# x loaded by pairs, a reordered beginning, and unread TensorE products, in an adaLN block on one core

## The chip, the cores and the metric

The kernel runs on one NeuronCore of one Trainium2 chip. The metric is the device time of one execution, in microseconds (us). Time before: 280.03 us, the median of 3 runs (278.7 to 280.95).

## The reference, cut to what matters

x has 16 batches ("blocks" below) of 256 tokens with 128 features. A condition vector gives each block a shift, a scale and a gate for attention and for the linear layer.

```python
mod = (_silu(c) @ wmod).reshape(16, 6, 1, -1)        # sa, ca, ga, sb, cb, gb
h = _layernorm(x) * (1 + ca) + sa
qkv = h @ W_qkv + b_qkv                              # 16 heads of 8 features
attn = softmax(einsum('bqhe,bkhe->bqhk', q, k)) / sqrt(128)
x = x + ga * (einsum('bihv,bvhd->bihd', attn, v) @ W_out + b_out)
h = _layernorm(x) * (1 + cb) + sb
x = x + gb * (quantised(h) @ quantised(w).T + bias)  # fp6 grid, blocks of 32
```

ga and gb are first pushed away from zero to at least 0.25 in magnitude.

## The kernel before, in words

All 16 blocks go through one software pipeline of `STEPS` (b = -2 to 18), each of 16 steps s. In step (b, s) TensorE computes the *second* scores of block b, head s (`scores2`, L1014, k as rows, into `ps_p2`), for which ScalarE takes the exponential (`exponentials`, L645), and the *first* scores of the head that lies LEAD = 20 steps ahead (`scores1`, L999, into the three banks of `ps_p1`), of which VectorE only takes each row's maximum (`maxima`, L822). The negated maxima are split by GpSimd (`split_max`), transposed by TensorE (L1058), copied to `maxT` by ScalarE (L637) and placed by two DMAs into two spare rows of `q_rows` (`place_max`, L409), so that the second scores come out with the maximum subtracted. Block 0's first scores thus begin at b = -2, s = 12; from there to b = 0 only first scores run (the lead phase).

For block c = b + 3, iteration b also prepares x: `transpose_x` (L1038), ScalarE's modulation into hT (`save_hT`, L615), q and k products (`project_qk`, L1051), ScalarE's copy (L626), GpSimd's split in a high and a low part (L515, L517). SyncE stores these parts to DRAM (`store_part`, L363) and loads them back in the layout that the scores want (`lay_out`: q_rows L375, k_rows L380; k_rows takes two DMAs, u = 0 and 1, for each half r). Blocks 0 and 1 are prepared ahead of the loop with `first_qk` (ScalarE, L620) and `first_low_part` (VectorE, L755). The LayerNorm statistics of x come from VectorE (`stats1`, L743, and `aggregate1`, L749 with L737 and L738), for block b + 5 in steps 6 and 7 of iteration b; those of blocks 3 and 4 in iterations -2 (s = 13, 14) and -1. Values (L1029), the output projection (L1082), LayerNorm 2 and the quantised linear layer (`transpose_hd` L1090, `linear` L1096) of a block follow in the next two iterations. The last block has a chain of its own (`..._last`; its last transposes L1120 and products L1124).

Each engine carries out its own list in order. SyncE's list is written by hand (L386 to L469): loads, the first stores and layouts, and then per iteration b: modb of block b + 1 (`load_modb`, L416), `place_max(b + 1, 0)`, the output of block b - 3 (L421), the two stores and the two layouts of block b + 3, `place_max(b + 1, 1)`. x is loaded in five transfers: blocks 0 and 1 by ScalarE, 2 and 3 early (L403), 4 and 5 behind the stores of block 1 (L435), and blocks 6 to 15 in one of 1280 KB ahead of the loop (L451). TensorE's list, ahead of its loop: the transpose of c, the modulation products, block 0's transpose and projections, block 1's transpose and projections, then the product of the 16 x 512 modulation rows (L1135), and `wf_d` and bias products (L1138, L1139), and block 2's transpose. ScalarE copies the modulation rows behind `first_qk` of block 1. VectorE carries out the weight's quantisation, the statistics of block 2, `first_low_part` of block 1, the operations on the modulation rows (L804 to L810), and the attention bias (L814).

Of the kernel before, what the change touches and what calls it, by code (L numbers as in the profile page):

```python
# [63 lines left out]
def adaln_block(nc, x, w_qkv, b_qkv, w_out, b_out, w_ffn, b_ffn, cond, w_mod, out):  # L64
# [4 lines left out]
    with ExitStack() as ctx:  # L69
# [147 lines left out]
        x_in = [sem("x0_in"), sem("x1_in"), sem("x2_x3_in"), sem("x4_x5_in"), sem("x_rest_in")]  # L217
# [99 lines left out]
        def x_ready(c):  # L317
            return (x_in[c if c < 2 else c // 2 + 1 if c < 6 else 4], 16)
# [47 lines left out]
        def lay_out(eng, c, kind, halves=range(2)):  # L366
# [4 lines left out]
            for r in halves:  # L371
# [5 lines left out]
                else:  # L377
                    for u in range(2):
# [8 lines left out]
        def _(sp):  # L387
# [15 lines left out]
            sp.dma_start(x_all[:, 2:4, :, :], x_tok[:, 2:4]).then_inc(x_in[2], 16)  # L403
# [24 lines left out]
            for r in range(2):  # L428
                lay_out(sp, 0, 0, (r,))
                lay_out(sp, 0, 1, (r,))  # L430
# [4 lines left out]
            sp.dma_start(x_all[:, 4:6, :, :], x_tok[:, 4:6]).then_inc(x_in[3], 16)  # L435
            sp.wait_ge(rows_ready, 1)
            sp.dma_start(mod_rows_dram, mod_rows[:, :, :].rearrange("b a n -> b (a n)")).then_inc(rows_stored, 16)
            for r in range(2):
                lay_out(sp, 1, 0, (r,))
                lay_out(sp, 1, 1, (r,))  # L440
            place_max(0, 0)
# [9 lines left out]
            sp.dma_start(x_all[:, 6:NB, :, :], x_tok[:, 6:NB]).then_inc(x_in[4], 16)  # L451
            for b in range(NB + 3):
# [14 lines left out]
                if has(b + 1):  # L467
                    place_max(b + 1, 1)
            sp.wait_ge(out_stored, 16 * NB)  # L469
# [125 lines left out]
        def _(act):  # L595
# [68 lines left out]
            first_qk(1, 0, q_full)  # L664
            first_qk(1, 1, k_full)
            act.wait_ge(rows_full, 1)
            act.activation(mod_rows[:, 1, :], rows_psum[:, 1, :], ACT.Copy)
            act.activation(mod_rows[:, 2, :], rows_psum[:, 2, :], ACT.Copy, bias=1.0).then_inc(rows_copied, 1)
            act.wait_ge(const_full, 1)
# [50 lines left out]
        def _(dve):  # L720
# [63 lines left out]

            dve.wait_ge(weights_loaded, 16 * 4)
# [12 lines left out]
            stats1(FIRST)  # L798
            aggregate1(FIRST)
            first_low_part(1, 0)  # L800
            first_low_part(1, 1)

# [10 lines left out]
            dve.wait_ge(wfT_copied, 1)  # L813
            dve.tensor_tensor(attn_bias[:, :], ps_post[:, E:2 * E], bout_bc[:, :], ALU.add).then_inc(const_ready, 1)  # L814
# [124 lines left out]

            for b in STEPS:  # L940
                for s in range(16):
# [20 lines left out]
                    if s == (13 if b == -2 else 6) and in_steps(b + 5):  # L962
                        stats1(b + 5)
                    if s == (14 if b == -2 else 7) and in_steps(b + 5):
# [15 lines left out]
        def _(pe):  # L980
# [260 lines left out]
```

## Time and profile before

| what | value |
|---|---|
| median of 3 runs | 280.03 us (278.7 to 280.95) |
| the profiled execution, own time | 277.82 us |
| its span in the profile | 275.8 us |
| TensorE busy | 256.1 us, 93% |
| VectorE busy | 232.6 us, 84% |
| ScalarE busy | 207.0 us, 75% |
| GpSimd busy | 185.8 us, 67% |
| moved by DMA | 35.45 MB, mean 129 GB/s |
| granted TensorE clock, mean | 0.945 |

The profile is of one execution; its times count from the start of the span. PE is TensorE (PEld its weight loads, which overlap it), DVE VectorE, ACT ScalarE, POOL GpSimd, SP SyncE; a q behind a name (SPq) is the engine's issuing of DMAs. "out<-in" names the tiles by the program's names without numbers, so `ps_p` stands for ps_p1, ps_p2 and ps_post or ps_pre where a line says so. The granted clock is a share of 2.4 GHz: 1.00, or 0.50 for 1.2 GHz. The recorded clock begins with its first event at 16.6 us, and a share of 1.00 before that is no reading.

### The profile page before, as it was taken

Reading aid. Unit: us, or ns where it says so; the run is one execution under the profiler, and the core shown is the slowest. Engines: PE = TensorE matmul, PEld = TensorE weight load, DVE = VectorE, ACT = ScalarE, POOL = GpSimd, SP = SyncE. Lnnn points to the kernel's source line nnn. Section 1 sums busy time; section 2 is a strip of 40 time slices with the busy share of each in tenths; the row PEclk is TensorE's granted clock in tenths of the full one; section 3 lists DMA queues with packets and bytes.
Section 4 is the critical chain, followed back from the end, with each engine's and each line's share of the span. In section 5 each row is a group of like instructions: output and inputs, shape, how many; then the busy total and the mean of one; then the engine's idle time right before and its main releaser. Section 6 shows DMA issues by size and latency. Waiting matters only on the chain.

```text
span 275.8 us, 7500 instructions
## 1 busy us (share of the span) xinstructions
PE 256.1 (93%) x2538; PEld 167.5 (61%) x2538; DVE 232.6 (84%) x597; ACT 207.0 (75%) x414; POOL 185.8 (67%) x384
## 2 busy tenths in 40 slices
PE   2789999999999999999999999999999989899952
PEld 2447656566666667666666666666767656565631
DVE  6679868889999999999999999999998978953264
ACT  5436867869797979888888889797979767878620
POOL 5724071558788878788887979797978653728450
PEclk9995559999999999999999999999999979999995
DMA  5476477555263536364626263726273440100001
GB/s 140 138 224 195 127 211 252 157 154 155 68 186 107 186 104 187 94 174 110 192 86 190 92 198 92 179 104 194 89 187 106 140 152 24 40 24 25 0 22 37
DMA packets 21205, 35.45 MB, mean 129 GB/s; under 512 B 3344, under 2 KB 16928, under 8 KB 19120
## 3 DMA queue, kind: packets, MB, share of 16 engines
q1 hardware_dynamic: 20592, 34.46, 42.5%
q10 hardware_dynamic: 576, 0.52, 0.6%
q8 instruction: 20, 0.33, 0.5%
q14 instruction: 17, 0.14, 0.2%
HBM read 23.93 MB, written 10.52 MB: 125 GB/s over the span
## 4 chain that ended last, share of the span: by engine, by line
PE 80%; DVE 6%; DMA 5%; SPq 3%; issue 3%; POOL 1%; ACT 1%; POOLq 0%; ACTq 0%; DVEq 0%
PE ps_p L999 29%; PE ps_o L1029 21%; PE ps_pre L1051 6%; PE ps_p L1014 4%; PE ps_post L1082 4%; PE ps_pre L1045 3%; PE ps_o L1068 3%; PE ps_post L1096 3%; PE ps_pre L1058 3%; DVE neg_max L822 2%; PE ps_pre L1038 2%; PE ps_post L1090 2%; DMA q_dram<-qk_parts 2%; PE ps_post L1076 1%; SPq L380 1%
## 5 line engine op out<-in xcount | busy, mean ns | idle before, releaser
L822 DVE TENSOR_REDUCE neg_max<-ps_p 128x2 f32<-128x512 f32 x256 | 164.2, 680 | 15.4 <-PE ps_p L999 14.0
L645 ACT ACTIVATE probs<-ps_p 128x512 f32<-128x512 f32 x256 | 139.2, 596 | 21.1 <-PE ps_p L1014 16.6
L999 PE MATMUL ps_p<-k_rows,q_rows 62*128 62x256 f32 x512 | 103.1, 324 | 2.8 <-DVE neg_max L822 1.6
L1014 PE MATMUL ps_p<-q_rows,k_rows 64*128 64x256 f32 x512 | 100.4, 315 | 1.5 <-DMA q_rows<-maxT 1.1
L999 PEld LDWEIGHTS ps_p<-k_rows,q_rows 62*128 62x128 f32 x512 | 74.2, 198 | 32.0 <-DVE neg_max L822 12.9
L1014 PEld LDWEIGHTS ps_p<-q_rows,k_rows 64*128 64x128 f32 x512 | 71.7, 190 | 5.2 <-ACT probs L645 2.8
L1029 PE MATMUL ps_o<-probs,v_aug 128*32 128x256 f32 x1024 | 70.0, 392 | 0.3 <-ACT probs L645 0.3
L1029 PEld LDWEIGHTS ps_o<-probs,v_aug 128*32 128x32 f32 x1024 | 27.1, 110 | 20.7 <-issue 1.6
L495 POOL CAST max_parts<-neg_max 128x16 fp32r<-128x16 f32 x32 | 6.4, 199 | 45.3 <-DVE neg_max L822 45.3
L517 POOL TENSOR_TENSOR qk_parts<-qk_full_sb,qk_parts 128x256 fp32r<-128x256 f32 x28 | 20.5, 731 | 2.3
L1051 PE MATMUL ps_pre<-hT,wqk_sb 128*128 128x256 f32 x56 | 19.2, 426 | 0.0
L637 ACT ACTIVATE maxT<-ps_pre 16x256 fp32r<-16x256 f32 x32 | 11.7, 365 | 6.6 <-PE ps_pre L1058 6.6
L626 ACT ACTIVATE qk_full_sb<-ps_pre,bqkv_col 128x256 f32<-128x256 f32 x28 | 13.2, 473 | 3.9 <-PE ps_pre L1051 3.8
L346 POOL TENSOR_TENSOR hq<-h,rs 128x256 fp8e4<-128x256 f32 x15 | 9.3, 617 | 8.7 <-DVE rs L868 8.7
L522 POOL TENSOR_TENSOR rstd<-ve,minus_half 128x2 f32<-128x2 f32 x16 | 11.2, 702 | 5.4 <-DVE ve L738 5.4
L515 POOL CAST qk_parts<-qk_full_sb 128x256 fp32r<-128x256 f32 x28 | 11.3, 403 | 5.3 <-ACT qk_full_sb L626 5.3
L329 POOL TENSOR_SCALAR xh<-x,nm,rstd 128x128 f32<-128x128 f32 x30 | 13.2, 452 | 1.6
L502 POOL TENSOR_TENSOR rstd<-ve,minus_half 128x2 f32<-128x2 f32 x16 | 11.2, 700 | 4.0 <-DVE ve L738 4.0
L354 POOL TENSOR_SCALAR xhat<-x_all,nm,rstd 128x128 f32<-128x128 f32 x28 | 12.3, 452 | 1.5
L550 POOL TENSOR_TENSOR x_res<-x_all,bias_b 128x256 f32<-128x256 f32 x16 | 11.8, 736 | 1.3
L335 POOL TENSOR_TENSOR xm<-xh,modb 128x256 f32<-128x256 f32 x15 | 11.1, 737 | 1.3
L339 POOL TENSOR_TENSOR h<-xm,modb 128x256 f32<-128x256 f32 x15 | 11.0, 735 | 1.2
(135 smaller groups left out, 347.9 us busy)
## 6 DMA issues: line engine op xcount, KB each, us to landing
q_rows<-q_dram SPq DMA_DIRECT2D x32, 256.0 KB
k_rows<-k_dram SPq DMA_DIRECT2D x64, 128.0 KB
q_dram<-qk_parts SPq DMA_DIRECT2D x32, 128.0 KB, 2.4
modb<-mod_rows_dram SPq DMA_DIRECT2D x16, 256.0 KB, 3.4
k_dram<-qk_parts SPq DMA_DIRECT2D x30, 128.0 KB, 2.4
out_dram<-out_sb SPq DMA_DIRECT2D x16, 128.0 KB, 1.8
x_all<-in_L_attn_x_dram SPq DMA_DIRECT2D x1, 1280.0 KB, 8.6
q_rows<-maxT SPq DMA_DIRECT2D x64, 8.0 KB
```

The costliest lines, as they stand in the source:

```text
L329: ins = eng.tensor_scalar(xh2[:, n, :], x1[:, n, :], nm2[:, n:n + 1], rstd2[:, n:n + 1], ALU.add, ALU.mult)
L354: ins = eng.tensor_scalar(xhat[:, c % 2, n, :], x_all[:, c, n, :], nm1[:, c % 2, n:n + 1], rstd1[:, c % 2, n:n + 1], ALU.add, ALU.mult)
L517: pool.tensor_tensor(qk_parts[:, c % 2, kind, 1, :], qk_full_sb[:, kind, :], qk_parts[:, c % 2, kind, 0, :].bitcast(F32), ALU.subtract).th ...
L550: pool.tensor_tensor(x_res[:, b % 2, :, :], x_all[:, b, :, :], bias_b[:, :].unsqueeze(1).to_broadcast([P, QT, E]), ALU.add).then_inc(x_res ...
L626: act.activation(qk_full_sb[:, kind, :], ps_pre[:, :], ACT.Identity, bias=bqkv_col[:, kind:kind + 1]).then_inc(saved, 1)
L637: act.activation(maxT[:, half, :], ps_pre[0:16, 0:T], ACT.Copy).then_inc(maxT_saved, 1)
L645: act.activation(probs[:, v % 2, u % 4, :], ps_p2[:, (16 * b + u) % P2_BANKS, :], ACT.Exp).then_inc(exp_done, 1)
L822: dve.tensor_reduce(neg_max[:, half, :, r, j], ps_p1[:, (16 * b + s) % P1_BANKS, :].rearrange("p (q k) -> p q k", q=QT), AX_X, ALU.max, ne ...
L999: ins = pe.matmul(ps_p1[:, (16 * b + s) % P1_BANKS, t * T:(t + 1) * T], q_rows[64 * r:64 * r + ROWS1, slot, i, t * P:(t + 1) * P], k_rows[ ...
L1014: ins = pe.matmul(ps_p2[:, (16 * b + u) % P2_BANKS, t * T:(t + 1) * T], k_rows[64 * r:64 * r + ROWS2, slot, i, t * P:(t + 1) * P], q_rows[ ...
L1029: ins = pe.matmul(ps_o[32 * j:32 * j + 32, half * T:(half + 1) * T], at[:, 2 * D * r:2 * D * r + 32], probs[:, v % 2, j, t * T:(t + 1) * T ...
L1051: pe.matmul(dst, wqk_sb[:, kind, :], hT[:, c % 3, :], start=True, stop=True).then_inc(full, 1)
```

## The change

Four things. (1) x is loaded by pairs of blocks: 4 and 5 behind the layouts of block 1, and 6 and 7 to 14 and 15 each at the end of SyncE's iterations b = 0, 2, ... 8. (2) ScalarE issues the u = 1 part of block 0's k_rows loads, and the store of the modulation rows goes ahead of block 1's stores. (3) Ahead of the loop, TensorE's rows product goes before block 1's projections, ScalarE copies those rows before `first_qk` of block 1, and VectorE takes the statistics of block 2 first, the rows' operations before `first_low_part` of block 1, and the statistics of block 3 behind it; those of block 4 go to iteration 0, the attention bias into the loop at b = -2, s = 13. (4) TensorE computes products that nobody reads: `awake` (identity by identity, fp32, 128 columns), `awake_wide` (512 columns, fp32r, into a bank of `ps_p2`, one or two for every two lead steps while b < 0: 15 in all), `awake_apart` (8 in the tail) and `unread` (a 256-column product into `ps_pre`, three in all). Its wait for `ident_r` and for all four `first_low` parts moves ahead of the loop.

```diff
@@ load conditions @@
-        x_in = [sem("x0_in"), sem("x1_in"), sem("x2_x3_in"), sem("x4_x5_in"), sem("x_rest_in")]
+        x_in = [sem("x0_in"), sem("x1_in")] + [sem(f"x{c}_x{c + 1}_in") for c in range(2, NB, 2)]
-        def lay_out(eng, c, kind, halves=range(2)):
+        def lay_out(eng, c, kind, halves=range(2), parts=range(2)):
...
-                    for u in range(2):
+                    for u in parts:
@@ block.sync @@
+            def load_x(c):
+                sp.dma_start(x_all[:, c:c + 2, :, :], x_tok[:, c:c + 2]).then_inc(x_in[c // 2 + 1], 16)
...
-                lay_out(sp, 0, 1, (r,))
+                lay_out(sp, 0, 1, (r,), (0,))
+            sp.wait_ge(rows_ready, 1)
+            sp.dma_start(mod_rows_dram, mod_rows[:, :, :].rearrange("b a n -> b (a n)")).then_inc(rows_stored, 16)
             sp.wait_ge(first_low, 3)
             store_part(sp, 1, 0)
             sp.wait_ge(first_low, 4)
             store_part(sp, 1, 1)
-            sp.dma_start(x_all[:, 4:6, :, :], x_tok[:, 4:6]).then_inc(x_in[3], 16)
-            sp.wait_ge(rows_ready, 1)
-            sp.dma_start(mod_rows_dram, mod_rows[:, :, :].rearrange("b a n -> b (a n)")).then_inc(rows_stored, 16)
             for r in range(2):
                 lay_out(sp, 1, 0, (r,))
                 lay_out(sp, 1, 1, (r,))
+            load_x(4)
             place_max(0, 0)
...
-            sp.dma_start(x_all[:, 6:NB, :, :], x_tok[:, 6:NB]).then_inc(x_in[4], 16)
             for b in range(NB + 3):
...
                 if has(b + 1):
                     place_max(b + 1, 1)
+                if b % 2 == 0 and b + 6 < NB:
+                    load_x(b + 6)
@@ block.scalar @@
             store_part(act, 0, 1, (1,))
-            first_qk(1, 0, q_full)
-            first_qk(1, 1, k_full)
             act.wait_ge(rows_full, 1)
...
+            first_qk(1, 0, q_full)
+            lay_out(act, 0, 1, (0,), (1,))
+            first_qk(1, 1, k_full)
+            lay_out(act, 0, 1, (1,), (1,))
@@ block.vector @@
             first_low_part(0, 1)
+            stats1(FIRST)
+            aggregate1(FIRST)
...
-            stats1(FIRST)
-            aggregate1(FIRST)
-            first_low_part(1, 0)
-            first_low_part(1, 1)
-
             dve.wait_ge(rows_copied, 1)
...
-            dve.wait_ge(wfT_copied, 1)
-            dve.tensor_tensor(attn_bias[:, :], ps_post[:, E:2 * E], bout_bc[:, :], ALU.add).then_inc(const_ready, 1)
+            first_low_part(1, 0)
+            first_low_part(1, 1)
+            stats1(FIRST + 1)
+            aggregate1(FIRST + 1)
...
-                    if s == (13 if b == -2 else 6) and in_steps(b + 5):
+                    if b == -2 and s == 13:
+                        bias_attention()
+                    if b == 0 and s == 1:
+                        stats1(4)
+                    if b == 0 and s == 2:
+                        aggregate1(4)
+                    if s == 6 and b >= 0 and in_steps(b + 5):
                         stats1(b + 5)
-                    if s == (14 if b == -2 else 7) and in_steps(b + 5):
+                    if s == 7 and b >= 0 and in_steps(b + 5):
                         aggregate1(b + 5)
@@ block.tensor @@
+            def awake(n):
+                for _ in range(n):
+                    pe.matmul(ps_p1[:, 0, 0:P], ident[:, :], ident[:, :], start=True, stop=True)
...
+            def awake_wide(n):
+                for _ in range(n):
+                    pe.matmul(ps_p2[:, 0, :], ident_r[:, :], qk_parts[:, 1, 0, :, :].rearrange("p u t -> p (u t)"),
+                              start=True, stop=True)
...
+            def unread(b):
+                wait(pe, (maxT_saved, 2 * (b + 1)))
+                pe.matmul(ps_pre[:, :], wqk_sb[:, 0, :], hT[:, LAST % 3, :], start=True, stop=True)
...
+            awake(1)
             transpose_x(0)
+            awake(1)
...
             project_qk(0, 1, k_full, ps_p2[:, 1, 0:T])
+            awake(2)
             transpose_x(1, (hT_saved, 1))
+            pe.wait_ge(wmod_rows_loaded, 16)
+            pe.matmul(ps_o[0:NB, :], cT[:, :], wmod_sb[:, 2 * E:6 * E], start=True, stop=True).then_inc(rows_full, 1)
             project_qk(1, 0, q_full, ps_p2[:, 0, 0:T], (first_low, 1))
             project_qk(1, 1, k_full, ps_p2[:, 1, 0:T], (first_low, 2))
...
+            awake(2)
...
             transpose_x(FIRST, (hT_saved, FIRST))
+            awake(6)
+            pe.wait_ge(ident_r_ready, 1)
+            pe.wait_ge(first_low, 2 * FIRST)
...
+                    if b < 0 and has1(b, s):
+                        awake_wide(2 if b == -1 and s in (0, 2, 4, 10, 12) else 1)
...
+                        if b - 1 == LAST:
+                            pe.wait_ge(max_done, 16 * NB)
+                            awake(2)
...
+                        awake(1)
...
+                    if s in (2, 4) and b == LAST - 2 or s == 4 and b == LAST - 1:
+                        unread(b)
...
                         linear(b - 2)
+                        awake_apart(8)
```

## Rows read from the trace of the kernel before

**Rows 1.** The page: busy time of each engine; the chain that ended last, by engine.
```profile
PE 256.1 (93%) x2538; PEld 167.5 (61%) x2538; DVE 232.6 (84%) x597; ACT 207.0 (75%) x414; POOL 185.8 (67%) x384
...
PE 80%; DVE 6%; DMA 5%; SPq 3%; issue 3%; POOL 1%; ACT 1%; POOLq 0%; ACTq 0%; DVEq 0%
```

**Rows 2.** Stretches: us, length, busy PE PEld DVE ACT POOL, granted clock, DMA share, GB/s.
```profile
16.60:20.00 3.40, 2.49 (x12) 1.66 (x12) 2.82 (x8) 0.91 (x2) 0.47 (x2) 0.98 0.80 257
20.00:31.50 11.50, 11.17 (x41) 8.47 (x40) 11.00 (x27) 8.10 (x7) 4.15 (x10) 0.50 0.65 188
31.50:39.10 7.60, 7.60 (x44) 5.02 (x42) 4.96 (x9) 5.58 (x12) 3.26 (x8) 0.50 0.55 150
39.10:49.20 10.10, 9.96 (x116) 5.85 (x114) 8.25 (x18) 7.25 (x16) 2.84 (x7) 0.94 0.74 233
49.20:53.10 3.90, 3.90 (x35) 2.87 (x34) 3.26 (x7) 3.90 (x9) 1.79 (x5) 1.00 0.65 183
53.10:64.40 11.30, 10.22 (x122) 6.15 (x120) 10.36 (x27) 7.74 (x17) 7.87 (x17) 1.00 0.54 159
111.10:125.30 14.20, 14.20 (x162) 9.40 (x158) 13.72 (x36) 12.08 (x26) 11.80 (x25) 1.00 0.44 128
218.00:233.80 15.80, 15.04 (x154) 9.47 (x154) 12.69 (x30) 10.92 (x23) 8.24 (x19) 0.89 0.32 103
233.80:248.10 14.30, 13.55 (x145) 8.80 (x145) 11.09 (x27) 10.96 (x23) 7.93 (x17) 1.00 0.09 31
267.00:271.00 4.00, 0.00 (x0) 0.00 (x0) 3.64 (x17) 0.00 (x0) 0.70 (x1) 0.76 0.11 35
```

**Rows 3.** The chain that ended last, before the first scores: start, us, what.
```profile
13.14 0.81 SPq L380
...
14.01 3.46 DMA k_rows<-k_dram
```

**Rows 4.** Timeline of TensorE, 7 to 26 us: start, us, instructions merged.
```profile
7.43 2.04 PE L1051 MATMUL ps_p<-hT,wqk_sb 128*128 128x256 f32 x4 [0.81 <-ACT hT L615]
...
18.17 0.70 PE L1051 MATMUL ps_pre<-hT,wqk_sb 128*128 128x256 f32 x2
...
25.43 1.22 PE L999 MATMUL ps_p<-k_rows,q_rows 62*128 62x256 f32 x4
```

**Rows 5.** Timeline of VectorE in the lead phase.
```profile
19.25 0.47 DVE L743 BATCH_NORM_STATS2 st<-x_all 128x6 f32<-128x128 f32 x2
19.65 0.67 DVE L822 TENSOR_REDUCE neg_max<-ps_p 128x2 f32<-128x512 f32 x1
20.24 0.23 DVE L749 BATCH_NORM_AGGREGATE mv<-st 128x2 f32<-128x6 f32 x2
...
20.67 4.86 DVE L822 TENSOR_REDUCE neg_max<-ps_p 128x2 f32<-128x512 f32 x8
...
28.57 3.68 DVE L822 TENSOR_REDUCE neg_max<-ps_p 128x2 f32<-128x512 f32 x6 [0.43 <-PE ps_p L999]
```

**Rows 6.** The chain that ended last, in block 0.
```profile
43.44 4.25 DMA q_dram<-qk_parts
```

**Rows 7.** Timeline of SyncE and VectorE around statistics, blocks 3 and 5.
```profile
81.05 0.32 SPq L416 DMA_DIRECT2D modb<-mod_rows_dram  x1
82.88 0.48 DVE L743 BATCH_NORM_STATS2 st<-x_all 128x6 f32<-128x128 f32 x2
...
108.80 0.32 SPq L416 DMA_DIRECT2D modb<-mod_rows_dram  x1
111.33 0.47 DVE L743 BATCH_NORM_STATS2 st<-x_all 128x6 f32<-128x128 f32 x2
```

**Rows 8.** DMA issues: count, KB each, median us from issue to landing.
```profile
modb<-mod_rows_dram SPq DMA_DIRECT2D x16, 256.0 KB, 3.4
...
x_all<-in_L_attn_x_dram SPq DMA_DIRECT2D x2, 256.0 KB, 4.6
x_all<-in_L_attn_x_dram ACTq DMA_DIRECT2D x2, 128.0 KB, 2.4
```

**Rows 9.** Timeline of TensorE in the tail.
```profile
266.13 0.71 PE L1096 MATMUL ps_p<-wf_b,hdT 128*128 128x128 f32 x4
...
272.07 1.22 PE L1124 MATMUL ps_p<-last_wf,hdT 128*128 128x128 f32 x4 [0.15 <-ACT hdT L649]
```

More of the change, by code:

```diff
@@ L317, in x_ready @@
         def x_ready(c):
-            return (x_in[c if c < 2 else c // 2 + 1 if c < 6 else 4], 16)
+            return (x_in[c if c < 2 else c // 2 + 1], 16)
         def in_steps(c):
@@ L402, in _ @@
                              ).then_inc(weights_loaded, 16)
-            sp.dma_start(x_all[:, 2:4, :, :], x_tok[:, 2:4]).then_inc(x_in[2], 16)
+            def load_x(c):
+                sp.dma_start(x_all[:, c:c + 2, :, :], x_tok[:, c:c + 2]).then_inc(x_in[c // 2 + 1], 16)
+            load_x(2)
             def place_max(b, half):
@@ L938, in finish_last, with bias_attention @@
                     ins.then_inc(out_ready, 1)
+            def bias_attention():
+                dve.wait_ge(wfT_copied, 1)
+                dve.tensor_tensor(attn_bias[:, :], ps_post[:, E:2 * E], bout_bc[:, :], ALU.add).then_inc(const_ready, 1)
             for b in STEPS:
@@ L980, in _, with awake_apart @@
         def _(pe):
+            def awake(n):
+                for _ in range(n):
+                    pe.matmul(ps_p1[:, 0, 0:P], ident[:, :], ident[:, :], start=True, stop=True)
+            def awake_apart(n):
+                for _ in range(n):
+                    pe.matmul(ps_o[:, 0:P], ident[:, :], ident[:, :], start=True, stop=True)
+            def awake_wide(n):
+                for _ in range(n):
+                    pe.matmul(ps_p2[:, 0, :], ident_r[:, :], qk_parts[:, 1, 0, :, :].rearrange("p u t -> p (u t)"),
+                              start=True, stop=True)
             pe.wait_ge(ident_ready, 1)
+            awake(2)
             pe.wait_ge(c_loaded, 16)
             pe.transpose(ps_pre[:, 0:NB], c_sb[:, :], ident[0:NB, 0:NB]).then_inc(c_full, 1)
+            awake(3)
             pe.wait_ge(cT_ready, 1)
@@ L1130, in _ @@
             project_qk(0, 1, k_full, ps_p2[:, 1, 0:T])
+            awake(2)
             transpose_x(1, (hT_saved, 1))
+            pe.wait_ge(wmod_rows_loaded, 16)
+            pe.matmul(ps_o[0:NB, :], cT[:, :], wmod_sb[:, 2 * E:6 * E], start=True, stop=True).then_inc(rows_full, 1)
             project_qk(1, 0, q_full, ps_p2[:, 0, 0:T], (first_low, 1))
             project_qk(1, 1, k_full, ps_p2[:, 1, 0:T], (first_low, 2))
-            pe.wait_ge(wmod_rows_loaded, 16)
-            pe.matmul(ps_o[0:NB, :], cT[:, :], wmod_sb[:, 2 * E:6 * E], start=True, stop=True).then_inc(rows_full, 1)
+            awake(2)
             pe.wait_ge(bv_ready, 1)
@@ L1166, in _ @@
                         project_qk(FIRST, 1, k_full, ps_pre[:, :], (q_saved, 1))
+                    if b < 0 and has1(b, s):
+                        awake_wide(2 if b == -1 and s in (0, 2, 4, 10, 12) else 1)
                     if s == 0 and has(b - 1):
                         values(b - 1, 3)
+                        if b - 1 == LAST:
+                            pe.wait_ge(max_done, 16 * NB)
+                            awake(2)
                     if s == 0 and pre:
```

## The prediction

> **What bounds the kernel now.** I read the engines' busy line and the chain that ended last first [rows 1]: TensorE is busy 93% of the span and VectorE 84%, and the chain runs over TensorE for 80%. So it is a TensorE kernel on average; but the change touches only the beginning, the x loads and the end, so I cut the span into stages [rows 2] and read each for itself. What the reader should see there: a block of the steady part (111.10:125.30) takes 14.2 us at a granted clock of 1.00 (2.4 GHz), with VectorE busy 13.72 of it: both engines are nearly full. Before that, from 20.0 to 40.2 us, the granted clock is 0.50 (1.2 GHz). It fell after a stretch in which TensorE was idle for 0.9 of 3.4 us (16.60:20.00), and came back at about 40, after a stretch (31.50:39.10) in which it was busy back to back. It fell again near 225 (0.89 in 218.00:233.80) and at 269, in a stretch where TensorE has nothing (267.00:271.00).
>
> Then who is last in each stretch. (a) Up to the first scores at 17.5 us the chain is q and k going to DRAM and back: the issue of two k_rows loads from 13.14 and the landing of the second at 17.47 [rows 3]. (b) In the lead phase (17.5 to 31.5, only first scores) VectorE sets the pace although TensorE runs at the lower level: eight maxima stand end to end in 4.86 us, six in 3.68 us, 0.60 us apart [rows 5], and a score step of two products takes TensorE 1.22/2 = 0.61 us even at the lower level [rows 4]. (c) In block 0 (31.50:39.10 and 39.10:49.20) VectorE is busy 13.2 of 17.7 us, so the low clock does cost. (d) Block 1 (49.20:53.10 and 53.10:64.40) takes 15.2 us at full clock: SyncE's queue is late, because the store of q waited 4.25 us for DMA engines full of the 1280 KB x load [rows 2, 6].
>
> **The change part by part.** Durations are those of the profiled execution, which took 277.82 us (span 275.8). That is 2.2 under the median of 280.03, below all three timed runs.
>
> *Start.* The chain into the first scores is 0.81 (the issue that stands ahead) + 3.46 (from issue to landing of the second k_rows load) [rows 3]. ScalarE now issues the second copy of each k_rows load, so SyncE's issues of 0.8 us no longer stand in a row: worth up to 0.8. Against it: ScalarE issues after its copy of q of block 1, which now stands behind the rows product (512 columns, so some 2 us at the lower level by the 2.04 of two 256-column projections) and two unread products, and its copy of k stands behind its own issue, with the store of k behind that. With six unread products before the loop (128 columns, half of a 256-column projection: 0.5 us each at the lower level, 0.3 at the upper) the start can also come later. The clock in the record stands at 1.00 in the first 16 us, but 2.04 us for two 256-column projections at 7.43, against 0.70 for one at 18.17, says the engine ran at the lower level [rows 4]. Busier from 7.4 us on, it should rise sooner. Bounds: 2.5 later (all fillers at the lower level) to 1.1 earlier; I take 0.3 earlier. The rows' operations on VectorE are only reordered; the statistics of block 3 (0.8 us) come before the first maximum and are covered by the landing of 3.46, in which VectorE has only small work.
>
> *Lead phase.* The statistics of blocks 3 and 4 leave it (4's go to block 0). A set costs 0.40 (the maximum behind the statistics at 19.25 starts at 19.65) plus 0.43 (20.24 to 20.67) [rows 5]: 2 x 0.82 = 1.6. VectorE's idle 0.43 at 28.1, a wait for scores held up by the value projection at 1.2 GHz, goes too: 2.1 us. Fifteen unread 512-column products come into the ten step pairs. Each streams twice the columns of a score product; at the upper level a pair is 0.73 (four score products, about the time at 17.51) + 0.25 to 0.5 against 1.2 for two maxima. So VectorE covers them, if the clock holds. If it doesn't, see the rivals.
>
> *Block 0.* Its first six steps took 7.6 us (31.5 to 39.1), the same steps of block 1 at the upper level 3.9 with more in them [rows 2]. Its rest took 10.1 at a mean clock of 0.94, so about 1.1 us of it at the lower level, of which half, some 0.6 us, was too much. The sum would be 7.6 - 3.9 + 0.6 = 4.3; the statistics of block 4 (0.8) now stand among six maxima (3.6), 0.4 more than TensorE's 3.9. I take 4.0. Bounds: 0 (the clock stays low) to 4.7.
>
> *Block 1.* 15.2 against 14.2 [rows 2]: the late store (4.25 [rows 6] against 2.4 for 128 KB elsewhere [rows 8]) held up the layout, and the row maxima that scores of block 1 wait for are queued behind it. By pairs, 256 KB stand before the store and not 1280: 1.0 us. Bounds 0 to 1.2.
>
> *x by pairs, the price.* The load of x for blocks b + 6 and b + 7 (256 KB, 0.4 us of SyncE) is issued at the end of SyncE's iteration b (b = 0, 2, ... 8), behind the last place_max, where the modb load now is issued; statistics of block b+6 are wanted at step 6 of block b+1. On VectorE they stand in the row of maxima: a late x stops everything there, TensorE's first scores two steps on. In block 5, SyncE is at that place at 108.75 (modb itself goes at 108.80), and the statistics start at 111.33; in block 3 they stand at 81.0 and 82.88 [rows 7]. The landing is the disputed number [rows 8]: a 256 KB load at this very place (modb) lands after 3.4 us, two 256 KB x loads in the busy beginning after 4.6, two 128 KB ones after 2.4. With 3.4, VectorE waits 0.8 us in blocks 5, 7, 9, and 1, and 1.5 in block 3. A block gives back some 0.4 (VectorE is busy 13.7 of 14.2), leaving 4 x 0.4 + 1.1 = 2.7 us lost. Bounds: with 2.4 nothing but 0.1; with 4.6, 4 x 1.6 + 2.3 = 8.7. I take 3.4, since it is the same size, queue and place.
>
> The Trainium skill, "DMA: Bandwidth & Descriptors", section "Anatomy of one DMA", fits a transfer as 2.0 us fixed plus its bytes over 436 GB/s. By it 256 KB would land after an estimated 2.6 us and VectorE would wait next to nothing; the trace's 3.4 disagrees. The term would be about 0.2 by the page and is 2.7 by the row.
>
> *The dip at 225.* Block 13 takes 15.8 against 14.3 for block 14 [rows 2]: 1.5 us, of which the two added 256-column products at steps 2 and 4 take back 0.1 (VectorE is the slower one there). 1.4. Bounds: -0.3 to 1.5, as the dip depends on where it falls.
>
> *Tail.* Eight unread products follow the projections of block 15 and run while VectorE works alone (267 to 271), so the last transposes and products find the upper level: the last linear pass took 1.22, the one before it 0.71 [rows 9], and the two transposes ahead of it, half as many columns, lose some 0.3: 0.8. The three other fillers stand mostly in waits for ScalarE and VectorE, at 0.25 each 0.3 show. 0.5. Bounds -0.5 to 0.8.
>
> Sum: 0.3 + 2.1 + 4.0 + 1.0 - 2.7 + 1.4 + 0.5 = 6.6 us, so 271.2 for an execution like the profiled one. The timed median lies 2.2 above it; part of that is where the clock falls, which the fillers should narrow, so I carry half: **272.3 us**.
>
> **Rivals.** A: the forecast.
> B: x comes late in earnest, 4.6 us per landing. Price 8.7 in place of 2.7: 278.3. For it: SyncE issues without a pause there and q_rows and k_rows are still in flight; against: modb at the same place lands in 3.4.
> C, the one on the other side: the fillers do not hold the clock in the lead phase, and TensorE becomes its bound. At the lower level 20 score steps x 0.61 = 12.2, two projections and the value product at 1.02 each [rows 4] and about 1 for the transposed maxima, 4.1 in all, and 15 fillers x 0.5 (twice the columns of a score product, 0.43, and its weights) = 7.5: 23.8 where 14.0 are there now, 9.8 more, with block 0 as slow as before. 277.82 + 9.8 + 2.7 - 0.3 - 1.0 - 1.4 - 0.5 = 287.1, and 288.2 with the half offset. It decides from the first 20 us: the clock must be up when the scores start. For it: it fell at 20.0 with TensorE busy 2.5 of 3.4 us. Against: the fillers stream more columns than the scores do.
> D: the clock is held only in the lead phase (where it is worth little) and block 0's 4.0 do not come, because the clock falls on its start or SyncE's queue of stores and layouts becomes what it waits for: 276.3. Against it: block 0 has VectorE and TensorE time to spare at the upper level, and SyncE starts its layouts earlier by what the lead phase gains.
> E: x lands in time (2.4, as the 128 KB loads do) and the start gives its 1.1 in place of 0.3: 272.3 - 2.6 - 0.8 = 268.9. For it: only five small gaps have to close. Against it: 3.4 at the same place. The Trainium skill's fit above speaks for it too.
>
> **Chances.** A 0.50, B 0.10, C 0.07, D 0.17, E 0.16. A measurement of this kernel can tell about 1% from no change (three runs lie within 0.8%), so faster means under 277.2. A, D and E are: 0.83. B is within 1%: 0.10. C is slower: 0.07. The range, 267.5 to 278.5, takes in A, D, E and most of B, and leaves out C.
>
> **What would show it.** Granted clock 1.00 from about 15 us to the end of block 0, and VectorE's maxima 0.60 apart with no gap from 17 to 29: right for the lead. Block 0 in 13 to 14 us, block 1 in 14.2 to 15. VectorE idle before its statistics (BATCH_NORM_STATS2 released by the DMA of x_all) in odd blocks 1 to 9, 0.8 us each, right for the price; nothing there means E, 2 us means B. Clock 1.00 at 225 and in the last transposes. Wrong: first scores later than 18.5 us, or a granted clock of 0.50 between 17 and 31 us with VectorE waiting for scores (C).

## The result and the profile after

| | before | after |
|---|---|---|
| timed median | 279.37 us (276.76 to 280.95, 4 runs) | 291.76 us (287.53 to 298.75, 4 runs) |
| ratio | | 1.0376, 95% interval 1.0253 to 1.0499 |
| profiled execution, own time | 277.82 us | 298.75 us |
| its span | 275.8 us | 297.0 us |

The change made the kernel slower, where 272.3 us and faster had been forecast. The profiled execution of the changed kernel is the slowest of these four; two further executions took 290.02 and 300.11 us. A second profiled one (`after_again`, below) took 291.03 us, and what is said here to recur is in both. Here and below a median is of all executions of a batch, and a ratio compares only those within 1.5% of the fastest of their kernel, since most kernels here, the one before too, have some slower executions.

The page of the changed kernel, busy time and chain, against [rows 1], and the granted clock in 40 slices of 7.4 us:

```profile
PE 280.1 (94%) x2615; PEld 183.6 (62%) x2615; DVE 232.3 (78%) x597; ACT 207.4 (70%) x414; POOL 185.4 (62%) x384
...
PEclk9975555999999999989999999999999999997598
...
PE 65%; DMA 10%; DVE 9%; SPq 7%; issue 4%; POOL 2%; ACT 1%; POOLq 0%; DVEq 0%; ACTq 0%
```

VectorE's work is the same to 0.3 us, TensorE has 24 us more of busy time, and the share of transfers (DMA) in the chain has doubled. The stretches against [rows 2] (us, length, busy PE PEld DVE ACT POOL, granted clock, DMA share, GB/s):

```profile
14.00:18.50 4.50, 1.57 (x15) 1.37 (x12) 2.30 (x10) 1.21 (x3) 0.00 (x0) 1.00 0.57 178
18.50:42.50 24.00, 23.85 (x69) 15.62 (x69) 13.09 (x21) 8.89 (x8) 4.60 (x11) 0.50 0.39 117
42.50:50.00 7.50, 7.50 (x41) 4.97 (x40) 4.97 (x13) 5.36 (x11) 2.82 (x7) 0.50 0.46 119
58.50:75.00 16.50, 14.49 (x152) 9.03 (x152) 12.23 (x31) 11.62 (x25) 7.02 (x16) 1.00 0.60 170
104.00:118.30 14.30, 14.30 (x162) 9.51 (x161) 13.82 (x36) 12.18 (x27) 11.89 (x25) 1.00 0.43 127
118.30:136.80 18.50, 16.23 (x160) 10.14 (x160) 13.40 (x36) 12.11 (x26) 12.76 (x26) 0.91 0.61 185
266.00:283.00 17.00, 16.66 (x111) 9.86 (x111) 3.59 (x13) 9.80 (x20) 8.59 (x15) 0.70 0.03 10
```

The lead phase is 24.0 us long, all of it at 0.50, with TensorE busy for 23.85 and VectorE for only 13.09. Before it TensorE has 1.57 us of work in 4.5. A steady block takes what it took (14.3 against 14.2), block 1 takes 16.5 and block 5 18.5, and the last block, 266.0 to 283.0, runs at a mean clock of 0.70.

To see where the 21.2 us of span went, I read in both timelines when each block's first exponential starts:

```
                                        before    after   after_again
first maximum                             18.05    19.44     19.37
first maximum to first exponential        14.4     23.9      23.9
block 0, exponential to exponential       15.2     15.7      15.3
block 1                                   15.05    16.7      15.7
blocks 3, 5, 7, 9, sum less 4 x 14.2       0.1      5.9       3.9
block 13                                  15.8     14.3      14.3
last block, first to last exponential     12.2     16.6      12.2
last exponential to the end               14.5     13.8      13.8
```

The start gives 1.4 more, the lead phase 9.5, blocks 0 and 1 2.1, the odd blocks 5.8, the last block 4.4, some 0.3 stand in block 2; 1.5 come back in block 13 and 0.7 at the end: 21.3 against 21.2. In the second execution the clock was up in the last block, and its span is 13.4 us over the one before the change.

**The start and the lead phase.** The chain (start, us, what) against [rows 3], then the timeline of TensorE against [rows 4]:

```profile
10.79 2.34 DMA k_dram<-qk_parts
13.13 0.02 issue
13.15 5.36 DMA k_rows<-k_dram
18.51 0.14 issue
```

```profile
14.06 1.50 PE L1001 MATMUL ps_p<-ident 128*128 128x128 f32 x12
18.65 1.19 PE L1034 MATMUL ps_p<-k_rows,q_rows 62*128 62x256 f32 x4 [3.08 <-DMA k_rows<-k_dram]
19.76 1.22 PE L1086 MATMUL ps_pre<-hT,wqk_sb 128*128 128x256 f32 x2
20.42 0.99 PE L1011 MATMUL ps_p<-qk_parts,ident_r 128*128 128x512 f32 x1
...
24.07 1.22 PE L1034 MATMUL ps_p<-k_rows,q_rows 62*128 62x256 f32 x4
25.22 1.22 PE L1011 MATMUL ps_p<-qk_parts,ident_r 128*128 128x512 f32 x2
26.37 1.22 PE L1034 MATMUL ps_p<-k_rows,q_rows 62*128 62x256 f32 x4
```

From about 12 us on the work ahead of the loop is done at the upper level (block 1's projections take 1.13 us from 12.10, where block 0's, of the same size, took 2.05 from 7.42), and it is over at 15.6 (twelve instructions, six unread products, in 1.50 us). Then TensorE waits 3.08 us for k_rows, and as the first scores begin the clock is down: four score products take 1.19 where they took 0.73. From there a pair of steps is 2.30 us with two fillers (24.07 to 26.37), 1.15 for scores and 1.15 for fillers, where VectorE needs 1.2. VectorE's timeline, against [rows 5], shows who waits:

```profile
22.17 1.29 DVE L829 TENSOR_REDUCE neg_max<-ps_p 128x2 f32<-128x512 f32 x2 [1.24 <-PE ps_p L1034]
24.90 1.29 DVE L829 TENSOR_REDUCE neg_max<-ps_p 128x2 f32<-128x512 f32 x2 [1.44 <-PE ps_p L1034]
27.20 1.29 DVE L829 TENSOR_REDUCE neg_max<-ps_p 128x2 f32<-128x512 f32 x2 [1.01 <-PE ps_p L1034]
```

**x by pairs.** SyncE issues the load for blocks 6 and 7 at 63.90, directly ahead of modb; VectorE stands before block 6's statistics for 3.08 us, against [rows 7] (timelines of SyncE and VectorE), and once more, the longest, in block 5; the median landing against [rows 8]:

```profile
63.90 0.39 SPq L405 DMA_DIRECT2D x_all<-in_L_attn_x_dram  x1
64.33 0.47 SPq L420 DMA_DIRECT2D modb<-mod_rows_dram  x1
...
68.22 0.49 DVE L750 BATCH_NORM_STATS2 st<-x_all 128x6 f32<-128x128 f32 x2 [3.08 <-DMA x_all<-in_L_attn_x_dram]
...
128.07 0.49 DVE L750 BATCH_NORM_STATS2 st<-x_all 128x6 f32<-128x128 f32 x2 [3.45 <-DMA x_all<-in_L_attn_x_dram]
```

```profile
x_all<-in_L_attn_x_dram SPq DMA_DIRECT2D x7, 256.0 KB, 4.3
```

This median of seven takes in the loads of blocks 2 and 3 (4.25 us) and 4 and 5 (5.30), which stand elsewhere. The five at the new place landed after 4.30, 2.83, 4.60, 2.96 and 3.52 us.

**The tail.** The eight unread products run while VectorE works alone, and the last linear pass takes 0.71 us in place of 1.22 [rows 9]:

```profile
288.54 1.95 PE L1006 MATMUL ps_o<-ident 128*128 128x128 f32 x16
...
293.78 0.71 PE L1159 MATMUL ps_p<-last_wf,hdT 128*128 128x128 f32 x4 [0.16 <-ACT hdT L654]
```

### The profile page after: what moved, and what is told of

It is laid out like the page before. It is cut to its first block, busy times and chain, and to the rows that moved or that the text cites. A ratio compares the mean times of both kernels' runs of the same rounds, so it can differ in the third digit from the quotient of the medians.

```text
span 297.0 us, 7660 instructions
## 1 busy us (share of the span) xinstructions
PE 280.1 (94%) x2615; PEld 183.6 (62%) x2615; DVE 232.3 (78%) x597; ACT 207.4 (70%) x414; POOL 185.4 (62%) x384
## 4 chain that ended last, share of the span: by engine, by line
PE 65%; DMA 10%; DVE 9%; SPq 7%; issue 4%; POOL 2%; ACT 1%; POOLq 0%; DVEq 0%; ACTq 0%
PE ps_p L1034 21%; PE ps_o L1064 16%; DVE neg_max L829 5%; PE ps_pre L1086 4%; DMA x_all<-in_L_attn_x_dram 4%; PE ps_p L1049 4%; DMA q_dram<-qk_parts 3%; PE ps_p L1011 3%; SPq L380 3%; SPq L413 3%; PE ps_post L1117 2%; PE ps_post L1131 2%; PE ps_pre L1093 2%; DMA k_rows<-k_dram 2%; PE ps_o L1103 2%
## 5 line engine op out<-in xcount | busy, mean ns | idle before, releaser
L1034 PE MATMUL ps_p<-k_rows,q_rows 62*128 62x256 f32 x512 | 106.2, 326 | 8.5 <-DVE neg_max L829 5.0
L1049 PE MATMUL ps_p<-q_rows,k_rows 64*128 64x256 f32 x512 | 103.4, 319 | 0.4 <-ACT probs L650 0.3
L1034 PEld LDWEIGHTS ps_p<-k_rows,q_rows 62*128 62x128 f32 x512 | 75.5, 201 | 42.1 <-DVE neg_max L829 19.7
L1049 PEld LDWEIGHTS ps_p<-q_rows,k_rows 64*128 64x128 f32 x512 | 73.2, 193 | 5.2 <-issue 2.6
L1064 PE MATMUL ps_o<-probs,v_aug 128*32 128x256 f32 x1024 | 72.6, 404 | 0.3 <-ACT probs L650 0.3
L1086 PE MATMUL ps_pre<-hT,wqk_sb 128*128 128x256 f32 x56 | 20.1, 443 | 0.0
L750 DVE BATCH_NORM_STATS2 st<-x_all 128x6 f32<-128x128 f32 x32 | 7.7, 281 | 8.2 <-DMA x_all<-in_L_attn_x_dram 8.1
L354 POOL TENSOR_SCALAR xhat<-x_all,nm,rstd 128x128 f32<-128x128 f32 x28 | 12.4, 451 | 1.5
L879 DVE TENSOR_TENSOR out_sb<-ps_post,x1b 128x256 f32<-128x256 f32 x14 | 5.8, 416 | 8.5 <-PE ps_post L1131 8.5
```

What stands on the lines that cost most here:

```text
L354: ins = eng.tensor_scalar(xhat[:, c % 2, n, :], x_all[:, c, n, :], nm1[:, c % 2, n:n + 1], rstd1[:, c % 2, n:n + 1], ALU.add, ALU.mult)
L1034: ins = pe.matmul(ps_p1[:, (16 * b + s) % P1_BANKS, t * T:(t + 1) * T], q_rows[64 * r:64 * r + ROWS1, slot, i, t * P:(t + 1) * P], k_rows[ ...
L1049: ins = pe.matmul(ps_p2[:, (16 * b + u) % P2_BANKS, t * T:(t + 1) * T], k_rows[64 * r:64 * r + ROWS2, slot, i, t * P:(t + 1) * P], q_rows[ ...
L1064: ins = pe.matmul(ps_o[32 * j:32 * j + 32, half * T:(half + 1) * T], at[:, 2 * D * r:2 * D * r + 32], probs[:, v % 2, j, t * T:(t + 1) * T ...
L1086: pe.matmul(dst, wqk_sb[:, kind, :], hT[:, c % 3, :], start=True, stop=True).then_inc(full, 1)
```

## The experiments

Two theories were put to the test. F: the fillers are the cost, since they stream at 1.2 GHz in the lead phase and TensorE becomes its bound. X: x by pairs comes late. Each run was timed beside runs of the kernel before on the same chip.

**The changed kernel again.** 

> The changed kernel once more, unchanged, to see which of its costs recur. Theory F (the fillers are what costs: they stream at 1.2 GHz in the lead phase and TensorE becomes its bound): the granted clock is 0.50 when the first scores start and 22 to 24 us pass from the first maximum to block 0's first exponential, against 14.4 before; where the clock is up instead, 14 to 16. Theory X (x by pairs comes late): VectorE idle before BATCH_NORM_STATS2 with the DMA of x_all as releaser, 5 to 8 us in sum over odd blocks. Both can hold; sum of both, 12 to 18 us over before.

One execution, 291.03 us. The phase from the first maximum to the first exponential is 23.9 us again, at the lower level from 17.5 us (TensorE stands still from 15.2 to 18.6), and VectorE waits 5.4 us in all for x. F and X both stand.

**Without the lead fillers.**

```diff
-                    if b < 0 and has1(b, s):
-                        awake_wide(2 if b == -1 and s in (0, 2, 4, 10, 12) else 1)
```

> The changed kernel without the 15 awake_wide products of the lead phase, all else kept. Theory F: the lead phase falls from about 24 to 13 to 15 us although the clock is still low in it, and the time from about 290 to 280 to 283. If the lead phase is long for another reason (late rows of k, statistics), it stays at 20 or more and the time stays within 3 us of the changed kernel's. Theory X: the waits for x stay as they are, 5 to 8 us in sum.

```profile
18.70:32.20 13.50, 13.14 (x52) 9.79 (x51) 11.81 (x20) 8.61 (x8) 4.61 (x11) 0.59 0.65 184
```

The stretch of the lead phase is 13.5 us at a mean clock of 0.59, against 24.0: F is right that the fillers make this phase long. They are not all of the difference, since the clock stayed up through the pause here and fell only at 21.1 us; the next run gives their price at one level. The profiled execution took 280.36 us, as expected. The other three took 285.13 to 290.0 (median of the four 287.45, before 278.13), which is worse than expected, with mean clocks of 0.928 to 0.936. They have no profile, so what they lost more is open. The waits for x in the odd blocks stay, 5.5 us in sum.

**Without any unread product.** All `awake`, `awake_wide`, `awake_apart` and `unread` calls are taken out.

> The changed kernel without any unread product (none at the start, in the lead phase, in block 13 and 14, or in the tail); the order of the beginning and x by pairs stay. Theory F: near the kernel without the lead fillers, 279 to 283, so the other fillers are worth under 2 us either way. If the fillers at the start held back the first scores, they come 1 us or more sooner here. Theory X: what is then left over before is the late x, 3 to 6 us.

283.39 us (278.96 to 285.51), a little over the range expected. The first maximum comes at 19.2 against 19.4: the fillers at the start hold nearly nothing back. VectorE waits 6.5 us in sum for x. The end takes 14.3 us from the last exponential, against 13.8 with the tail's fillers and 14.5 before.

```profile
18.30:34.10 15.80, 15.35 (x53) 11.23 (x54) 11.93 (x20) 8.63 (x8) 4.61 (x11) 0.50 0.55 160
```

Here, as in the changed kernel, the clock is down before the first scores start, so the two lead phases differ by the fillers at the same level: 23.9 against 15.8 us, 8.1 for fifteen, or 0.54 each. The rest of the 10 us between the changed kernel and the run without lead fillers goes with the 2.6 us of scores at the upper level there.

**x of blocks 6 to 15 in one transfer, all fillers kept.**

```diff
-                if b % 2 == 0 and b + 6 < NB:
-                    load_x(b + 6)
...
+            sp.dma_start(x_all[:, 6:NB, :, :], x_tok[:, 6:NB]).then_inc(x_in[4], 16)
```

> The changed kernel with blocks 6 to 15 of x in one transfer ahead of the loop again, all fillers kept. Theory X: no wait for x on VectorE in any block, and 5 to 8 us less than the changed kernel: 283 to 286. Theory F alone: within 2 us of the changed kernel, since the long lead phase (23 us) stays; the store of q in block 0 then waits for the 1280 KB again, some 1 us.

288.08 us, ratio 1.0348 (1.0244 to 1.0452), against 1.0376 (1.0253 to 1.0499) for the changed kernel. The medians are 3.7 us apart, less than X had it, and the intervals overlap almost wholly, so the times don't show what x costs. The profile does: no wait for x in a block is left, the odd blocks from 3 to 9 take 14.2 us each, and block 1 takes 15.1 in place of 16.7. The lead phase is long in this kernel too, although its first scores, from 18.0 us, start at the upper level after a pause of 2.61 us:

```profile
18.00:19.70 1.70, 1.69 (x8) 1.20 (x9) 1.18 (x2) 0.32 (x1) 0.00 (x0) 1.00 0.79 258
19.70:40.50 20.80, 20.80 (x62) 13.50 (x61) 11.89 (x20) 8.57 (x8) 4.60 (x11) 0.50 0.42 114
```

The clock fell after 1.7 us of scores and fillers without a gap. So with a pause of this length ahead, starting at the upper level was not enough here, and the fillers did not hold the clock.

**No pause ahead of the first scores.**

```diff
             transpose_x(FIRST, (hT_saved, FIRST))
-            awake(6)
+            awake(20)
```

> The changed kernel with 20 instead of 6 unread 128-column products between block 2's transpose and the first scores, so that TensorE has no 3 us pause there. Theory G (the pause of 3 us ahead of the first scores drops the clock, and fillers would hold it from there): the first scores start at the upper level, the granted clock stays 1.00 through the lead phase, and this phase takes 12 to 13 us in place of 24, the time falls to 276 to 281. Theory H (the lead phase's own load, scores paced by VectorE plus these fillers, doesn't keep the clock up): the clock falls within 4 us after the first scores all the same, and the time stays at 287 to 292. If the clock is low when the 20 products begin, they take 10 us and the first scores come 4 to 6 us later.

The timeline of TensorE in this kernel, and its stretches:

```profile
14.01 4.63 PE L1001 MATMUL ps_p<-ident 128*128 128x128 f32 x40
18.57 0.74 PE L1034 MATMUL ps_p<-k_rows,q_rows 62*128 62x256 f32 x4
...
22.95 0.73 PE L1034 MATMUL ps_p<-k_rows,q_rows 62*128 62x256 f32 x4
23.61 0.73 PE L1011 MATMUL ps_p<-qk_parts,ident_r 128*128 128x512 f32 x2
```

```profile
18.60:32.30 13.70, 13.70 (x70) 9.13 (x69) 12.50 (x21) 8.76 (x8) 4.63 (x11) 1.00 0.61 170
32.30:44.60 12.30, 12.27 (x129) 7.69 (x129) 11.62 (x29) 10.30 (x23) 6.06 (x14) 1.00 0.63 181
```

Theory G holds. Fourteen more unread products, in a wait that was there anyway, take the lead phase from 24.0 to 13.7 us with all fifteen lead fillers still in it, and block 0 to 12.3. The time is 279.69 us, ratio 0.9956 (0.9904 to 1.0008): 12 us less than the changed kernel. One of the ten executions took 1244.62 us, for a reason that is open; the others took 276.41 to 282.61. The phase that fillers made 8.1 us longer at the lower level is shorter with them, at the upper one, than the 14.4 of the kernel before. Two of them beside four score products make 1.33 us per pair (22.95 to 24.27), so VectorE's 1.2 is not quite reached. Twenty products are a few too many: the k_rows load landed at 18.0, and the products ended at 18.6.

**Only the x loads of the change, on the kernel before.** The beginning stays as it was; blocks 6 to 15 come in pairs at the end of iterations 0, 2, ... 8.

> The kernel before with only its x loads changed: blocks 6 to 15 in pairs at the end of SyncE's iterations 0, 2, ... 8, as in the change. Theory X (late x): VectorE waits for x in blocks 1, 3, 5, 9, 5 to 7 us in sum, and the time is 3 to 6 us over before, less the 1 us that block 1 gains. If the waits come from the changed beginning instead, none shows here and the time is that of before.

280.58 us, ratio 1.0029 (0.9976 to 1.0081), so 0.8 us over before, where 2 to 5 was expected. VectorE waits before the statistics in all five odd blocks, 4.1 us in sum (5 to 7 expected), two of them:

```profile
56.08 0.49 DVE L744 BATCH_NORM_STATS2 st<-x_all 128x6 f32<-128x128 f32 x2 [1.23 <-DMA x_all<-in_L_attn_x_dram]
84.58 0.49 DVE L744 BATCH_NORM_STATS2 st<-x_all 128x6 f32<-128x128 f32 x2 [0.44 <-DMA x_all<-in_L_attn_x_dram]
```

**The same pairs an iteration sooner.**

```diff
-            sp.dma_start(x_all[:, 6:NB, :, :], x_tok[:, 6:NB]).then_inc(x_in[4], 16)
+            sp.dma_start(x_all[:, 6:8, :, :], x_tok[:, 6:8]).then_inc(x_in[4], 16)
...
+                if b % 2 == 1 and b + 7 < NB:
+                    sp.dma_start(x_all[:, b + 7:b + 9, :, :], x_tok[:, b + 7:b + 9]).then_inc(x_in[(b + 7) // 2 + 1], 16)
```

> The kernel before with x by pairs issued about an iteration sooner: 6 and 7 ahead of the loop, where the 1280 KB stood, and b + 7 and b + 8 at the end of iterations 1, 3, 5, 7. Theory X: no wait for x, all of the cost of pairs_only gone, and block 1 a little shorter than before's 15.05 (the store of q not held up): 277 to 279 beside before's 278 to 280. If the pairs cost something besides their lateness (DMA engines shared with the layouts), blocks stay over 14.2 us here.

277.26 us, ratio 0.9969 (0.9916 to 1.0022). By the medians this is 3.3 us less than the pairs at their late place in the same batch of runs, by the ratios 1.7, with intervals that overlap a little. No wait for x is left, and block 1 takes 14.0 us from exponential to exponential, against 15.1 before. So no cost of the pairs themselves shows; their place had one.

**Only the changed beginning.** No unread product, x of blocks 6 to 15 in one transfer.

> The changed kernel without any unread product and with x of blocks 6 to 15 in one transfer: what is left is the changed beginning (ScalarE's k_rows issues, rows first, statistics moved). My theory of the start said 0.3 us sooner at the first scores and 2.1 us off the lead phase: 276 to 278. Rival, from the profiles seen so far: the four k_rows loads in flight together with the rest delay block 0's first half, so the first maximum comes 1 us later (19.1 to 19.5 against 18.1), and the sum is within 1 us of before.

281.19 us, ratio 1.0069 (1.0024 to 1.0113): 0.7% slower than before. The first maximum comes at 19.2. The lead phase takes 15.8 us although the statistics are out of it, since it now begins at the lower level, where the pairs with a projection take TensorE longer than VectorE (its timeline):

```profile
21.47 1.29 DVE L828 TENSOR_REDUCE neg_max<-ps_p 128x2 f32<-128x512 f32 x2 [0.81 <-PE ps_p L1031]
23.77 6.30 DVE L828 TENSOR_REDUCE neg_max<-ps_p 128x2 f32<-128x512 f32 x10 [1.01 <-PE ps_p L1031]
```

The rival named in the expectation was right on the late start; by its "within 1 us of before" it was short, since 0.7% is 1.9 us.

**The bridge and early pairs together.** `bridge` with the pairs issued as above.

> bridge (20 unread products before the first scores, lead fillers, tail fillers) with x by pairs issued an iteration sooner. If the waits for x (4.4 us in bridge) are the rest of the loss and add to the clock's gain: no wait for x, 3 to 4 us less than bridge, 275 to 277 beside before's 279. If they were hidden or another wait takes their place (modb, placed maxima): the same as bridge within 1 us.

273.41 us, ratio 0.9824 (0.9777 to 0.9872): by the ratios 3.7 us less than `bridge`, as expected, and under the 275 to 277 that had been named. No wait for x in a block is left. The two gains add. The profiled execution is the slowest of the six (277.71, the others 273.12 to 273.44): the clock fell at 251.6, in its last block, which took 15.2 us.

**With block 0's k_rows loads back on SyncE.**

```diff
-                lay_out(sp, 0, 1, (r,), (0,))
+                lay_out(sp, 0, 1, (r,))
...
-            lay_out(act, 0, 1, (0,), (1,))
...
-            lay_out(act, 0, 1, (1,), (1,))
...
-            awake(20)
+            awake(16)
```

> bridge_early with block 0's k_rows loads all on SyncE again, and 16 in place of 20 unread products before the first scores. If the change's first scores are late because ScalarE's issues put all k_rows loads in flight at once, the k_rows landing of the first half falls from 5.4 back to 3.5 us and the first maximum from 19.2 to about 18.2, 1 us less than bridge_early. If it is the earlier work ahead (the clock, hT) or the DRAM traffic of other stores, the first maximum stays at 19.2.

272.64 us (272.20 to 272.98, six runs), ratio 0.9800 (0.9757 to 0.9842): this version is faster than both kernels. The chain in it, and its lead phase and block 0:

```profile
14.18 3.57 PE ps_p L1000 x32
17.75 0.04 issue
17.80 0.71 PE ps_p L1033 x4
```

```profile
17.80:31.00 13.20, 13.20 (x65) 8.89 (x66) 12.02 (x20) 8.27 (x8) 4.61 (x11) 1.00 0.65 188
31.00:43.50 12.50, 12.47 (x130) 7.80 (x130) 11.82 (x29) 10.49 (x22) 6.03 (x14) 1.00 0.68 199
```

The first scores start at 17.8 against 18.7 in `bridge_early`, right behind the unread products; the first half of k_rows had landed at 17.7. Two things were changed here at once, and both count: in `bridge_early` this half landed at 18.05, and the first scores then waited until 18.7 for the unread products, four of which are gone here. All profiles together bear out that the place of the issue matters: this half landed at 17.88 to 18.51 in the eight with ScalarE's issues and at 17.17 to 17.66 in the six with SyncE's alone. Why is not shown. With ScalarE's issues all four k_rows loads and both q_rows loads are out by 15.5 us in place of 16.8, so the half that the scores wait for may share the DMA engines with the other; but the stores behind them are sooner too, and ScalarE's issue itself took 1.23 to 1.51 us where SyncE's second one takes 0.7.

**The same without lead fillers, and with one per pair.** `awake_wide` is taken out, or called with 1 throughout.

> sync_issue without the awake_wide products in the lead phase. Are these needed once there is no pause ahead of the first scores? If the scores alone keep the clock up: granted clock 1.00 through the lead phase and up to 1 us less than sync_issue, since pairs with two fillers take 1.33 us against 1.2. If the fillers are what holds it: the clock falls 2 to 6 us after the first scores, block 0's period returns to 14.7 to 15.3, and the time is 2 to 4 us over sync_issue.

> sync_issue with one awake_wide product per pair of lead steps everywhere (10 instead of 15). If one is enough to hold the clock, pairs fall from 1.33 to 1.2 us and the lead phase is 0.5 us shorter than sync_issue's; if it is too little, the clock falls in the lead phase in some or all runs and the time is 1 us or more over sync_issue's.

Without them: 276.60 us (273.14 to 282.38), ratio 0.9875 (0.9835 to 0.9914), by the medians 4.0 us over `sync_issue` and by the ratios 2.1. The clock, up at the first scores, goes down 6 us later:

```profile
17.80:23.80 6.00, 4.92 (x24) 3.26 (x24) 4.96 (x9) 3.79 (x4) 2.25 (x4) 0.99 0.60 182
23.80:40.90 17.10, 16.74 (x84) 11.11 (x82) 14.06 (x32) 11.13 (x17) 6.63 (x17) 0.50 0.63 183
```

In this profiled execution the lead phase is 0.7 us and block 0 2.9 us longer than in `sync_issue`; another 2.9 us are lost in the last block, where the clock fell too.

With one per pair the profiled execution has the shortest lead phase of all, 12.4 us at 1.00, and 272.03 us; but of six runs three are at 278.99, 281.76 and 281.28, with mean clocks of 0.947 to 0.972 against 0.992 and more in its two fastest. The median is 276.59. So one filler is faster when the clock holds. That it is too few to hold it in the lead phase each time is likely but not shown: the three have no profile, and `bridge_early` shows that the clock can also fall in the last block, with all fifteen. The mean clocks of the two slowest, 0.947 and 0.950, are as low as the 0.950 of the execution above, in which it fell in both.

## Why the prediction was wrong

*The step that failed is the start.* It reads "Busier from 7.4 us on, it should rise sooner", and the lead phase's "VectorE covers them, if the clock holds" rests on it. The clock did rise sooner: it was up at about 12. But I did not follow where that work ends. Everything ahead of the loop got done by 15.6 us in place of 16.4, the first half of k_rows landed at 18.5 in place of 17.5, and the pause ahead of the first scores grew from 1.07 to 3.08 us. The clock fell at its end, and TensorE, busy 23.85 of 24.0 us, became the bound: the lead phase cost 9.5 us more, where 2.1 less was forecast. `bridge` fills the pause, and the clock holds. Rival C had the price and the sentence "the clock must be up when the scores start"; its chance of 0.07 was the mistake. That sentence is not the whole condition: in `x_rest` the clock was up when the scores started behind a pause of 2.61 us, and fell 1.7 us later. The argument against C, "the fillers stream more columns than the scores do", holds where no pause stands ahead (`sync_issue` against `sync_nowide`), and `x_rest` shows that it doesn't hold behind one.

*Rival C was what happened.* It had 23.8 us for the lead phase, measured 24.0, with 7.5 us for the fillers, measured 8.1. It had 288.2 for the whole, measured 291.76 (287.53 to 298.75), and this is partly luck: it took the x loads at 2.7 us and the start as a gain.

*Start, size.* Forecast 0.3 sooner, measured 1.4 later to the first maximum: 1.1 to the first scores, and 0.2 to 0.3 since they run at the lower level. The later landing goes with the issues moved to ScalarE. I had priced the issue slot (0.8 us) and taken the landing of 3.46 as given. ScalarE's issue began at 13.15, 0.86 sooner than SyncE's second one had, but took 1.51 us and ended at 14.66, where SyncE's had ended at 14.69: the slot was not won. The last piece landed 5.36 us after 13.15, later by 1.0 us than before.

*Lead phase and block 0, mechanism.* Right where the clock holds. From first maximum to first exponential 13.7 us in `sync_issue` against 14.4: 0.7 of the 2.1, since pairs of 1.33 with two fillers take the place of VectorE's 1.2 (a filler takes 0.33 there, two in 0.66, where the working had 0.25 to 0.5 per pair). Block 0's period falls from 15.2 to 12.3: 2.9 of the 4.0. A part of the lead phase's old pace was a gift too: in the kernel before, the first pairs ran at the upper level until 20.0, which `order_only` lost and so came out 1.4 us longer with less work on VectorE.

*Block 1.* 1.0 forecast, 1.0 measured in `pairs_early` (15.05 to 14.04). In the changed kernel the wait for x hides it.

*x by pairs.* Right in place and sign. In `pairs_only` VectorE waits 4.1 us in sum, where 4 x 0.8 + 1.5 = 4.7 stood in the working, and moving the load an iteration sooner is worth 3.3 us by the medians and 1.7 by the ratios, against the 2.7 forecast. In the changed kernel the waits in odd blocks are 7.9 and 5.4 us in two executions. The disputed landing was not what was mis-sized: at this place it was 3.4 us or less in `pairs_only` (median 3.1), and had a median of 3.5 and 3.2 in the two executions of the changed kernel, so rival B's 4.6 was reached only once (block 5). What the working had wrong there is when the load is issued: it counted 2.6 us from the issue to the moment when VectorE wants the statistics (1.9 in block 3), and in blocks 1 and 5 of the changed kernel only 1.2 were left (issue at 63.90, wanted at 65.14; 123.45 and 124.62). The fit that the prediction cites from the Trainium skill ("DMA: Bandwidth & Descriptors", "Anatomy of one DMA") gives an estimated 2.6 us; that section states it for DMAs issued by GpSimd, and these are issued by SyncE. Every landing at this place took longer, 2.66 to 4.60 us.

*Dip and tail.* The tail gets 0.7 shorter (14.5 to 13.8), forecast 0.5, in six of the nine profiles with its fillers. In `bridge_early`, `sync_nowide` and `sync_one` it takes 14.3, with the last linear pass at 1.22 us again: the fillers don't hold the clock there each time. Block 13 was at 14.3 in every profile with the `unread` products, which agrees with the forecast of 1.4, but this is not shown to be their doing. `no_unread`, `order_only` and `pairs_only`, which lack them, had no dip in block 13 either, two of these had one in block 14 instead, and in the changed kernel the clock fell in block 5, behind the longest wait for x, and in the last block (4.4 us more each, 3.45 of block 5's being the wait).

## What to carry to other kernels

An unread product that is nearly covered at the upper level made TensorE the bound at the lower one (8.1 us for fifteen). So the first question is not how much such a filler streams but what stands ahead of it: look for the longest pause there, and fill that wait first. Sooner work ahead of a fixed wait only lengthens the wait. And when a big load is cut into pieces, leave room before the reader of each: issued an iteration sooner they were never waited for here; at the late place, where VectorE waited, it wanted them 1.2 to 3.2 us after the issue, and they landed after 2.7 to 4.6.

## What the runs showed of the hardware that was not expected

- The same fifteen 512-column products cost 8.1 us at a granted clock of 0.50 (lead phase 23.9 us against 15.8 in `no_unread`). At 1.00 the step from ten to fifteen costs 0.7 (13.0 in `sync_one`, 13.7 in `sync_issue`).
- Scores that started at 1.00 behind a pause lost the clock soon after: 1.7 us later with fillers behind 2.61 us of pause (`x_rest`), 2.6 us later without them behind 2.78 (`no_lead_fill`). Behind no pause they kept it through the lead phase with fillers (`bridge`, `sync_issue`) and 6 us long without (`sync_nowide`).
- Issuing half of the loads of 128 KB each from a second queue brought the data that the scores wait for 0.2 to 1.3 us later (17.88 to 18.51 against 17.17 to 17.66), not sooner.
- The clock's record can be incomplete: in `pairs_only` it gives 1.00 for 18 to 34 us, while the value product takes 1.22 us, the time it has in the kernel before at 26.6 us with the clock at 0.50, against 0.60 in `bridge` at 1.00. Durations decide.

```profile
18.00:34.00 16.00, 15.66 (x59) 11.51 (x58) 13.94 (x33) 9.17 (x10) 4.62 (x11) 1.00 0.60 176
```

```profile
28.14 1.22 PE L1046 MATMUL ps_pre<-wqkv_sb,hT 128*128 128x128 f32 x4
```
